# First body's row numbers ahead of the order of the others, a semaphore for each gathered tile, GpSimd without its copies

## The chip, the cores and the metric

One core of a Trainium2 chip runs the kernel. The metric is the time on the device in microseconds (us), the median of three runs. The engines are named as in the profile: PE (TensorE, matmuls), PEld (its weight loads), DVE (VectorE), ACT (ScalarE), POOL (GpSimd), SP (the engine that only starts transfers). A letter q behind an engine's name (PEldq, POOLq) means its sequencer: register work, branches, waits.

## The reference

Two layers on 4 x 512 tokens of width 512, in float32:

```python
x = x + tanh(g_xattn) * xattn(ctx_512, layernorm(x), Wq, Wk, gamma_raw)
x = x + tanh(g_ffn)   * ffn(layernorm(x), gate_w, w1, w2, w3)
# xattn: sim = Q K^T; top 30% of each row kept; A = sigmoid(sim) * mask
#        A = (A + A^T) / 2;  (1 - gamma) * layernorm(x) + gamma * A
# ffn:   each token goes to its 2 best of 8 experts, with softmax weights
#        expert e: w2[e] @ (silu(w1[e] x) * (w3[e] x)), 512 -> 1024 -> 512
```

## The kernel before

The first part (to about 130 us) makes the attention layer, writes the rows with their routing data to a table `found` in HBM, and sorts the tokens by expert. The second part does the experts. Its matmuls take each operand as a high and a low float32r part, three matmuls for one product (L729 to L731).

Two tiles of 128 tokens of expert 0 are done by code written out (`for g in range(WRITTEN)`, g = 0 and 1). All others are done by *bodies*: a loop over experts, and in it a loop over bodies of two tiles of tokens (256 columns), or two and a half where a branch chooses the wide form (320 columns). A body has 8 chunks. Fifteen bodies run here. On PE the branch is `with pe.If(n == wide_at)` (L901): the wide body's code comes first, and the code of the narrow one lies behind it.

A body needs the row numbers of its tiles. PE counts them into PSUM bank 6 (`all_blocks`, L724). DVE turns them into row numbers for all bodies (`order_rows`, L1560 and L1566), copies those of each expert to the place where its bodies begin (`place_rows`, L1577; for experts 1 to 7 it first reads that place from a table), and hands the three row numbers of one body over in `rows_now` (`next_rows`, L1581). POOL waits for that, copies them (`rows_taken`, L525), drains, and starts three indirect DMAs (L528) that bring 128 rows each into `x_body`. All three count up one semaphore, `x_body_in`. ACT waits for all of them and normalises the three tiles (L1082), PE turns them (L754 the two full tiles, L760 the half one), ACT and DVE split the result into high and low parts (L1087, L1092, L1593, L1598), and the last of these sets `xT_body_set`, for which the body's first matmul waits.

For the first body this chain runs beside the second written tile (g = 1). PE's order there is fixed: the turning stands ahead of the last six matmuls of the tile's second layer. `tabulate` on DVE makes the table of bounds that every engine loads before it enters the loops (`table_set`; L331 is that load). SP begins to load expert 1's weights, three transfers of 2 MB (L384), when the first body's rows are there. The results of a body are added to the output by indirect DMAs of POOL (L516 for the written tiles, L534 for bodies); ahead of them it copies the tokens' rows too (`y_row`, L514, L541) and drains (L542).

Of the kernel before, what the change touches and what calls it, by code (L numbers as in the profile page):

```python
# [25 lines left out]
I32 = mybir.dt.int32  # L26
U32 = mybir.dt.uint32
# [4 lines left out]
P = 128  # L32
# [43 lines left out]
FIRST, END, PAIR_TURN, WIDE_AT, THIRD_AT, WIDE_TURN, FRESH_AT, WIDE_SO_FAR, WIDE_IN_ALL = range(9)  # L76
ENTRIES, ENTRY_ROW = 9, 12


def build(nc, x, xT, ctxT, wq_rows, wk_rows, gateT, weights, gains, out):  # L80
# [10 lines left out]
    with stack:  # L91
# [18 lines left out]
        y_row = sb("y_row", [P, 3], I32)  # L110
        no_shift = sb("no_shift", [P, 3], I32)
# [4 lines left out]
        rows_taken = sb("rows_taken", [P, 3], I32)  # L116
# [84 lines left out]
        early_row = sb("early_row", [P, 1], F32, part1)  # L201
        blk_i = sb("blk_i", [P, E], I32, part1)
# [52 lines left out]
        body_rows = scratch[:, TB * N:TB * N + E * BODY_ROWS]  # L255
        row_shift = scratch[:, TB * N + E * BODY_ROWS:TB * N + E * BODY_ROWS + 3 * PLACES].rearrange("p (j c) -> p j c", j=3)
# [13 lines left out]
        UP_BODY, Y_BODY, X_BODY, X_ENTRY, X_LAST = 1, (4, 5, 3), (6, 7), (6, 3), 0  # L270
# [52 lines left out]
        rows_set, x_body_in, x_body_set = sem("rows_set"), sem("x_body_in"), sem("x_body_set")  # L323
# [4 lines left out]
        def entries(eng, e, needed=(FIRST,)):  # L328


            _, values = nc.values_load_multi_w_load_instructions(table[0:1, bass.ds(e * ENTRY_ROW, ENTRIES)], engines=[eng.engine], min_val=0, max_val=MOST,  # L331
                                                                   skip_runtime_bounds_check_because="tabulate() counts bodies, of which there are fewer than MOST")
            bounded = {FIRST: MOST - 1, WIDE_SO_FAR: E}
# [5 lines left out]
        def _(sp):  # L339
# [46 lines left out]
            sp.wait_ge(x_body_in, 48)  # L386
# [4 lines left out]
        def _(pool):  # L391
# [4 lines left out]
            nc.gpsimd.memset(no_shift[:, :], 0)  # L396
# [21 lines left out]
            nc.gpsimd.memset(rows_at[:, :], 0.0)  # L418
# [93 lines left out]
            def add_y(g):  # L512
                pool.wait_ge(y_set, g + 1)
                nc.gpsimd.tensor_tensor(y_row[:, 0:1], token_out[:, 0:1], no_shift[:, 0:1], ALU.add)  # L514
                pool.drain()
                nc.gpsimd.indirect_dma_start(  # L516
                    out, bass.IndirectOffsetOnAxis(ap=y_row[:, 0:1], axis=0), y[:, :], None,
                    bounds_check=TOKENS + 3 * P - 1, oob_is_err=True, compute_op=ALU.add,
                ).then_inc(y_added, 16)

            def gather_body(n):
# [3 lines left out]
                nc.gpsimd.tensor_tensor(rows_taken[:, :], rows_now[:, :], no_shift[:, :], ALU.add)  # L525
                pool.drain()
                for j in range(3):
                    nc.gpsimd.indirect_dma_start(  # L528
                        x_body[:, j, :], None, found, bass.IndirectOffsetOnAxis(ap=rows_taken[:, j:j + 1], axis=0),
                        bounds_check=P + TOKENS + 2 * P - 1, oob_is_err=True,  # L530
                    ).then_inc(x_body_in, 16)

            def add_tile(j, rows, added):
                nc.gpsimd.indirect_dma_start(  # L534
                    out, bass.IndirectOffsetOnAxis(ap=y_row[0:rows, j:j + 1], axis=0), y_tiles[j][0:rows, :], None,
# [43 lines left out]
            pool.wait_ge(x_body_in, end * 48 + 48)  # L579
# [3 lines left out]
        def _(pe):  # L583
# [212 lines left out]
            for g in range(WRITTEN):  # L796
# [69 lines left out]
            with pe.Fori(0, E) as e:  # L866
# [3 lines left out]
                with pe.Fori(of[FIRST], of[END]) as n:  # L870
# [37 lines left out]
        def _(act):  # L908
# [921 lines left out]
```

## Time and profile before

| | us |
|---|---|
| median of three runs (769.46, 771.75, 771.84) | 771.75 |
| the profiled execution, its own time | 769.46 |
| its span, from the first to the last instruction | 767.7 |
| PE busy | 719.1 (94%) |
| DVE, ACT, POOL busy | 398.1, 332.6, 200.5 |

The span and all moments in the rows are those of one profiled execution; 1.8 us of its own time lie outside the span. Since PE is busy for 94% of the span, its idle stretches are what to look for. They lie in the first part, at the entry to the loops (178 to 196 us), and at the end, where POOL adds the last body's result.

### The profile page before, as it was taken

To read this page: it belongs to the slowest core of one execution; us is meant where nothing else is said; L and a number is where in the kernel's file an instruction comes from. 1 tells how busy PE (TensorE), PEld (TensorE's weight loads), DVE (VectorE), ACT (ScalarE), POOL (GpSimd) and SP (SyncE) were. 2 spreads that over 40 slices of the span, in tenths; PEclk is the share of its full clock that TensorE was granted. 3 is DMA by queue.
4 is the path that set the end of the run, shared out by engine and by line. 5 is a ranking of instruction groups with operands and counts; after the bars stand their busy time and mean duration, and the time that the engine had idled before them with its cause. 6 is when DMAs were issued, how large, how long until landed. Compare 5 with 4: busy or idle time off the path is not lost.

```text
span 767.7 us, 13122 instructions
## 1 busy us (share of the span) xinstructions
PE 719.1 (94%) x4507; PEld 620.1 (81%) x4509; DVE 398.1 (52%) x1013; ACT 332.6 (43%) x649; POOL 200.5 (26%) x243
## 2 busy tenths in 40 slices
PE   7698798795999999999999999999999999999994
PEld 3494443574989998999989989999999899989993
DVE  2787779884554355425443564254535542644312
ACT  4797485512454244333533353335333533544221
POOL 4203824972204110403030304030403040203111
PEclk9758999998999999999999999999999999999997
DMA  8972253417516340543226324432363244303122
GB/s 311 411 302 111 110 220 115 138 15 282 178 80 199 121 112 33 135 160 69 109 58 236 69 109 121 166 74 104 62 232 69 109 138 152 67 1 69 42 27 28
DMA packets 24231, 98.76 MB, mean 129 GB/s; under 512 B 4560, under 2 KB 4816, under 8 KB 20368
## 3 DMA queue, kind: packets, MB, share of 16 engines
q1 hardware_dynamic: 14496, 70.54, 23.9%
q0 software_dynamic: 9568, 27.96, 16.1%
q8 instruction: 9, 0.15, 0.1%
q14 instruction: 14, 0.11, 0.0%
q10 hardware_dynamic: 144, 0.00, 0.0%
HBM read 77.50 MB, written 20.99 MB: 128 GB/s over the span
## 4 chain that ended last, share of the span: by engine, by line
issue 67%; POOL 11%; DVE 8%; PE 7%; POOLq 3%; DMA 2%; DVEq 1%; ACT 1%; SPq 0%
POOL x_body L528 4%; POOL out L534 4%; DVE front L1204 2%; POOL xb L474 2%; PE bank L627 1%; PE bank L674 1%; DMA out<-xb 1%; PE bank L600 1%; POOLq L542 1%; PE bank L683 1%; POOLq L331 1%; DVE scratch L1179 1%; PE bank L672 1%; PE bank L590 1%; DMA front<-ctxT 1%
## 5 line engine op out<-in xcount | busy, mean ns | idle before, releaser
L729 PE MATMUL bank<-xT_body_hi,w_hi 128*128 128x256 f32 (+1 forms) x960 | 275.8, 287 | 3.9 <-issue 3.6
L731 PE MATMUL bank<-xT_body_lo,w_hi 128*128 128x256 f32 (+1 forms) x960 | 275.3, 287 | 0.8 <-issue 0.8
L730 PE MATMUL bank<-xT_body_hi,w_lo 128*128 128x256 f32 (+1 forms) x960 | 275.1, 287 | 0.0
L729 PEld LDWEIGHTS bank<-xT_body_hi,w_hi 128*128 128x128 f32 x960 | 181.1, 189 | 10.7 <-issue 5.4
L730 PEld LDWEIGHTS bank<-xT_body_hi,w_lo 128*128 128x128 f32 x960 | 181.5, 189 | 3.6
L731 PEld LDWEIGHTS bank<-xT_body_lo,w_hi 128*128 128x128 f32 x960 | 181.2, 189 | 0.0
L1735 DVE TENSOR_TENSOR h<-bank,act_g 128x256 f32<-128x256 f32 (+1 forms) x120 | 52.4, 437 | 207.5 <-PE bank L731 202.2
L1116 ACT ACTIVATE hT_hi<-h 128x256 fp32r<-128x256 f32 (+1 forms) x120 | 51.4, 428 | 165.6 <-DVE h L1735 165.6
L1369 DVE TENSOR_TENSOR w_lo<-raw,w_hi 128x1024 fp32r<-128x1024 f32 x88 | 105.2, 1223 | 25.0 <-ACT w_hi L958 25.0
L1112 ACT ACTIVATE act_g<-bank 128x256 f32<-128x256 f32 (+1 forms) x120 | 46.5, 388 | 162.2 <-PE bank L731 162.0
L729 PE MATMUL bank<-w_hi,hT_hi 128*128 128x512 f32 (+1 forms) x280 | 114.1, 408 | 1.9 <-DVE hT_lo L1648 1.8
L731 PE MATMUL bank<-w_lo,hT_hi 128*128 128x512 f32 (+1 forms) x280 | 110.2, 393 | 0.0
L730 PE MATMUL bank<-w_hi,hT_lo 128*128 128x512 f32 (+1 forms) x280 | 110.1, 393 | 0.0
L525 POOL TENSOR_TENSOR rows_taken<-rows_now,no_shift 128x3 int32<-128x3 int32 x16 | 3.0, 185 | 350.5 <-DVE rows_now L1581 350.5
L958 ACT ACTIVATE w_hi<-raw 128x1024 fp32r<-128x1024 f32 x88 | 89.1, 1044 | 0.1
L1740 DVE TENSOR_TENSOR hT_lo<-h,hT_hi 128x256 fp32r<-128x256 f32 (+1 forms) x120 | 52.5, 438 | 45.7 <-ACT hT_hi L1116 44.5
L731 PEld LDWEIGHTS bank<-w_lo,hT_hi 128*128 128x128 f32 (+1 forms) x280 | 51.6, 184 | 13.2
L729 PEld LDWEIGHTS bank<-w_hi,hT_hi 128*128 128x128 f32 (+1 forms) x280 | 51.6, 184 | 12.8 <-DVE hT_lo L1648 3.7
L528 POOL DMA_INDIRECT x_body<-found,rows_taken x48 | 51.4, 1070 | 32.3 <-issue 32.3
L730 PEld LDWEIGHTS bank<-w_hi,hT_lo 128*128 128x128 f32 (+1 forms) x280 | 51.8, 185 | 8.9
L1082 ACT ACTIVATE x_body<-x_body 128x512 f32<-128x512 f32 x48 | 35.4, 802 | 5.1 <-DMA x_body<-found,rows_taken 5.1
L534 POOL DMA_INDIRECT out<-y_body,y_row x18 | 35.2, 1954 | 5.5 <-issue 5.5
(307 smaller groups left out, 772.1 us busy)
## 6 DMA issues: line engine op xcount, KB each, us to landing
raw<-weights SPq DMA_DIRECT2D x24, 2048.0 KB, 10.4
raw<-xT SPq DMA_DIRECT2D x4, 1024.0 KB, 11.6
xb<-x SPq DMA_DIRECT2D x4, 1024.0 KB, 20.2
w_hi<-weights POOLq DMA_DIRECT2D x2, 2048.0 KB, 14.9
found<-xb SPq DMA_DIRECT2D x4, 1024.0 KB, 4.5
out<-xb SPq DMA_DIRECT2D x4, 1024.0 KB, 6.9
found<-scratch SPq DMA_DIRECT2D x1, 2092.0 KB, 30.2
front<-ctxT SPq DMA_DIRECT2D x4, 256.0 KB, 4.6
```

The lines of the kernel that those rows point to most:

```text
L528: nc.gpsimd.indirect_dma_start(x_body[:, j, :], None, found, bass.IndirectOffsetOnAxis(ap=rows_taken[:, j:j + 1], axis=0), bounds_check=P ...
L534: nc.gpsimd.indirect_dma_start(out, bass.IndirectOffsetOnAxis(ap=y_row[0:rows, j:j + 1], axis=0), y_tiles[j][0:rows, :], None, bounds_chec ...
L729: nc.tensor.matmul(out_ap, hi, hi_w, start=start, stop=False)
L730: nc.tensor.matmul(out_ap, lo, hi_w, start=False, stop=False)
L731: return nc.tensor.matmul(out_ap, hi, lo_w, start=False, stop=stop)
L958: nc.scalar.activation(w_hi[q][:, j, :], raw[:, q, j * OPW:(j + 1) * OPW], ACT.Copy).then_inc(hi_set[q], 1)
L1082: last = nc.scalar.activation(x_body[:, j, 0:D], x_body[:, j, 0:D], ACT.Identity, bias=x_body[:, j, SHIFT:SHIFT + 1], scale=x_body[:, j, S ...
L1112: nc.scalar.activation(act_g[:, k % 2, 0:cols], bank[GATE[k % 2]][:, 0:cols], ACT.Silu).then_inc(silu_chunk, 1)
L1116: nc.scalar.activation(h_chunk_hi[:, k % 3 * WIDE_COLS:k % 3 * WIDE_COLS + cols], h[:, k % 2, 0:cols], ACT.Copy).then_inc(h_chunk_high, 1)
L1369: V.tensor_tensor(w_lo[q][:, j, :], raw[:, q, j * OPW:(j + 1) * OPW], w_hi[q][:, j, :].bitcast(F32), ALU.subtract).then_inc(lo_set[q], 1)
L1735: V.tensor_tensor(h[:, k % 2, 0:cols], bank[UP_BODY][:, 0:cols], act_g[:, k % 2, 0:cols], ALU.mult).then_inc(h_chunk, 1)
L1740: V.tensor_tensor(h_chunk_lo[:, at], h[:, k % 2, 0:cols], h_chunk_hi[:, at].bitcast(F32), ALU.subtract).then_inc(h_chunk_set, 1)
```

## The change

The diff, cut to its core (the semaphores' and buffers' declarations and the renumbered constants are left out):

```diff
@@ table and entries: one number more for each expert
+FIRST, ..., WIDE_IN_ALL, ROWS_FROM = range(10)
+ENTRIES, ENTRY_ROW = 10, 12
-        rows_at = sb("rows_at", [P, 3 * (MOST + 2) + BODY_ROWS])
+        body_rows = sb("body_rows", [P, (E + 1) * BODY_ROWS], I16)
-        UP_BODY, Y_BODY, X_BODY, X_ENTRY, X_LAST = 1, (4, 5, 3), (6, 7), (6, 3), 0
+        UP_BODY, Y_BODY, X_BODY, X_ENTRY, X_LAST = 1, (4, 5, 3), (6, 7), (1, 3), 0
@@ SP
-            sp.wait_ge(x_body_in, 48)
+            sp.wait_ge(x_body_in[2], 16)
@@ POOL
             def add_y(g):
                 pool.wait_ge(y_set, g + 1)
-                nc.gpsimd.tensor_tensor(y_row[:, 0:1], token_out[:, 0:1], no_shift[:, 0:1], ALU.add)
-                pool.drain()
                 ... the indirect DMA, now with token_out
             def gather_body(n):
                 pool.wait_ge(rows_set, n + 1)
-                nc.gpsimd.tensor_tensor(rows_taken[:, :], rows_now[:, :], no_shift[:, :], ALU.add)
-                pool.drain()
+                pool.sem_inc(let, 1)
                 for j in range(3):
                     ... the indirect DMA, now with rows_now
-                    ).then_inc(x_body_in, 16)
+                    ).then_inc(x_body_in[j], 16)
             def add_body(n):
                 pool.wait_ge(y_set, n)
-                nc.gpsimd.tensor_tensor(y_row[:, :], token_out[:, :], no_shift[:, :], ALU.add)
-                pool.drain()
+                pool.sem_inc(let, 1)
@@ PE, the written tiles
-                    if k == OPS - 1 and g + 1 < WRITTEN:
+                    if k == OPS - 2 and g + 1 < WRITTEN:
                         transpose_x(nth + 1)
-                    elif k == OPS - 1:
+                    if k == OPS - 1 and g + 1 == WRITTEN:
                         pe.wait_ge(x_body_set, 1)
                         turn_pair(X_ENTRY)
+                        pe.wait_ge(x_third_set, 1)
                         turn_last()
@@ PE, in a body
                                 pe.wait_ge(x_body_set, next_nth)
+                                pe.wait_ge(x_third_set, next_nth)
                                 turn_pair(X_BODY)
@@ ACT
             def normal_body(n):
-                act.wait_ge(x_body_in, n * 48 + 48)
                 for j in range(3):
+                    act.wait_ge(x_body_in[j], n * 16 + 16)
                     last = nc.scalar.activation(...)
-                last.then_inc(x_body_set, 1)
+                    if j > 0:
+                        last.then_inc((x_body_set, x_third_set)[j - 1], 1)
@@ DVE
+            def entry_rows():
+                first = rows_ps[:, WRITTEN:WRITTEN + 3]
+                dve.wait_ge(rows_mm, 2)
+                V.scalar_tensor_tensor(entry_shift[:, :], first, 0.0, pad_row[:, :], ALU.is_equal, ALU.mult)
+                dve.drain()
+                V.scalar_tensor_tensor(rows_now[:, :], first, float(P - 1), entry_shift[:, :], ALU.add, ALU.add).then_inc(rows_set, 1)
-            def place_rows(experts):
-                ... a table load, a copy and a drain for each expert
-            def next_rows(n):
-                V.tensor_copy(rows_now[:, :], rows_at[:, bass.ds(n * 3, 3)]).then_inc(rows_set, 1)
+            def next_rows(body):
+                V.tensor_copy(rows_now[:, :], body_rows[:, bass.ds(body * 3, 3)]).then_inc(rows_set, 1)
@@ DVE, tabulate
+                V.scalar_tensor_tensor(rows_from, expert_no[:, :], float(BODY_ROWS // 3), first, ALU.mult, ALU.subtract)
+                V.memset(rows_from[:, 0:1], float(WRITTEN // 2))
@@ DVE, order of the calls
+            slots(0, range(PICKS // 2))
             x_low(2)
-            slots(0)
+            slots(0, range(PICKS // 2, PICKS))
             ...
             product(0, 2, 2 * OPS)
-            order_rows()
-            place_rows([0])
-            next_rows(0)
+            entry_rows()
             h_low(0, 2)
             product(1, 2, 2 * OPS)
             h_low(1, 2)
             tabulate()
-            place_rows([1])
             pair_low(0, 1, X_ENTRY)
             pair_low(1, 2, X_ENTRY)
             last_low(3)
+            order_rows()
             scale_y(0, 1, 2 * OPS)
-            place_rows(range(2, E))
@@ DVE, in a body
-                        next_rows(nth)
+                        next_rows(next_expert if turn else next_here)
```

DVE now works out the first body's three columns alone, and orders the rest after it has split the first body's tiles. On DVE, from the first product of the second written tile (L1644) on, before (`rows_mm` is PE's count of rows, `hhi_set` and `silu_set` are ACT's):

```order
L1644 TENSOR_TENSOR h<-bank,act_g 128x512 [waits piece_done0,silu_set0]
L1560 TENSOR_SCALAR scratch<-bank,pad_row 128x144 [waits rows_mm]
L1560 TENSOR_SCALAR scratch<-bank,pad_row 128x144 x2
L1561 MEMSET scratch 128x216
L1566 SCALAR_TENSOR_TENSOR scratch<-bank,scratch 128x72 x2
L1566 SCALAR_TENSOR_TENSOR scratch<-bank,scratch 128x8x8
L1577 COPY rows_at<-scratch 128x24
L1581 CAST rows_now<-rows_at 128x3
```

And now:

```order
L1644 TENSOR_TENSOR h<-bank,act_g 128x512 [waits piece_done0,silu_set0]
L1562 SCALAR_TENSOR_TENSOR entry_shift<-bank,pad_row 128x3 [waits rows_mm]
L1564 SCALAR_TENSOR_TENSOR rows_now<-bank,entry_shift 128x3
L1648 TENSOR_TENSOR hT_lo<-bank,hT_hi 128x512 [waits hhi_set0]
L1644 TENSOR_TENSOR h<-bank,act_g 128x512 [waits piece_done1,silu_set1]
L1648 TENSOR_TENSOR hT_lo<-bank,hT_hi 128x512 [waits hhi_set1]
```

Eight instructions from the product to `rows_now` have become three. Further on, on DVE from the end of the table to the second tile's output (L1653), before:

```order
L1552 CAST table<-scratch 1x9x8
L1576 TENSOR_LOAD table [waits table_set]
L1576 ISA x2
L1577 ISA
L1577 COPY rows_at<-scratch 128x27
L1593 TENSOR_TENSOR xT_body_lo<-bank,xT_body_hi 128x2x256 [waits x_body_hi] x2
L1598 TENSOR_TENSOR xT_body_lo<-bank,xT_body_hi 128x4x64 [waits x_body_hi]
L1653 TENSOR_SCALAR y<-bank,meta_now 128x512 [waits y_added,piece_done2]
```

And now:

```order
L1554 CAST table<-scratch 1x10x8
L1593 TENSOR_TENSOR xT_body_lo<-bank,xT_body_hi 128x2x256 [waits x_body_hi,table_set]
L1593 TENSOR_TENSOR xT_body_lo<-bank,xT_body_hi 128x2x256 [waits x_body_hi]
L1598 TENSOR_TENSOR xT_body_lo<-bank,xT_body_hi 128x4x64 [waits x_body_hi]
L1570 TENSOR_SCALAR scratch<-bank,pad_row 128x144 x3
L1575 SCALAR_TENSOR_TENSOR body_rows<-bank,scratch 128x72 x2
L1575 SCALAR_TENSOR_TENSOR body_rows<-bank,scratch 128x8x8
L1653 TENSOR_SCALAR y<-bank,meta_now 128x512 [waits y_added,piece_done2]
```

The table load and the copy are gone from between the table and the split, and the order of all rows stands behind the split. On POOL, from the first written tile's addition on, before:

```order
L514 TENSOR_TENSOR y_row<-token_out,no_shift 128x1 [waits y_set]
L516 DMA out<-y,y_row 2432x512
L525 TENSOR_TENSOR rows_taken<-rows_now,no_shift 128x3 [waits rows_set]
L528 DMA x_body<-found,rows_taken 128x523 x3
L514 TENSOR_TENSOR y_row<-token_out,no_shift 128x1 [waits y_set]
L516 DMA out<-y,y_row 2432x512
L556 UNCONDITIONAL_BRANCH [waits table_set]
```

And now (drains and semaphore steps are not in these lists):

```order
L513 DMA out<-y,token_out 2432x512 [waits y_set]
L524 DMA x_body<-found,rows_now 128x523 [waits rows_set]
L524 DMA x_body<-found,rows_now 128x523 x2
L513 DMA out<-y,token_out 2432x512 [waits y_set]
L551 UNCONDITIONAL_BRANCH [waits table_set]
```

The copies no longer stand between a wait and its DMAs.

## Rows read from the trace of the kernel before

**Rows 1.** Waits on PE, 150 to 200 us: total, times, longest.

```profile
PE bank L729 <- issue: 3.6, 1, 3.6
PE bank L754 <- ACT x_body L1082: 3.5, 1, 3.5
PE bank L731 <- issue: 0.8, 1, 0.8
```

**Rows 2.** Waits on PE from 195 us to the end, columns as above.

```profile
PE bank L754 <- ACT x_body L1082: 3.4, 4, 0.8
```

**Rows 3.** Timeline of PE: start, us, engine, line, operation, idle time before and releaser.

```profile
181.44 1.09 PE L754 MATMUL bank<-ident,x_body 128*128 128x128 f32 x8 [3.54 <-ACT x_body L1082]
182.47 0.54 PE L760 MATMUL bank<-ident,x_body 64*128 64x64 f32 x4
...
189.43 0.50 PE L729 MATMUL bank<-xT_body_hi,w_hi 128*128 128x256 f32 x1 [3.56 <-issue]
```

**Rows 4.** PE's sequencer by line: ns min/median/max, first and last start.

```profile
L866 PEldq MOVE  x1: 44/44/44, 181.5 to 181.5; - x1
L901 PEldq COMPARE_BRANCH  x18: 75/206/5947, 183.2 to 719.5; - x18
```

**Rows 5.** DMA queues, 182.7 to 186.7 us, the weights' own: packets, MB, share.

```profile
q1 hardware_dynamic: 119, 1.72, 102.2%
```

**Rows 6.** DMA queues, 186.7 to 189.4 us, the instruction queue alone.

```profile
q8 instruction: 1, 0.02, 2.2%
```

**Rows 7.** Timeline of DVE, columns as in rows 3.

```profile
157.06 0.17 DVE L1586 COPY meta_next<-xtile 128x8 f32<-128x8 f32 x1 [1.92 <-ACT xT_hi L1006]
...
157.98 4.39 DVE L1442 TENSOR_SCALAR scratch<-from_one,slot,number 128x128 f16<-128x128 f16 x16
...
168.72 0.92 DVE L1560 TENSOR_SCALAR scratch<-bank,pad_row 128x144 f32<-128x144 f32 x3 [0.67 <-PE bank L724]
...
170.80 0.17 DVE L1581 CAST rows_now<-rows_at 128x3 int32<-128x3 f32 x1
...
180.14 0.27 DVE L1552 CAST table<-scratch 1x72 int32<-1x72 f32 x1
...
183.21 1.29 DVE L1593 TENSOR_TENSOR xT_body_lo<-bank,xT_body_hi 128x512 fp32r<-128x512 f32 x2 [1.81 <-ACT xT_body_hi L1087]
184.41 0.42 DVE L1598 TENSOR_TENSOR xT_body_lo<-bank,xT_body_hi 128x256 fp32r<-128x256 f32 x1
```

**Rows 8.** Timeline of POOL at the first body's gathers and at the end.

```profile
172.76 1.10 POOL L528 DMA_INDIRECT x_body<-found,rows_taken  x1 [1.52 <-issue]
...
175.49 1.01 POOL L528 DMA_INDIRECT x_body<-found,rows_taken  x1 [0.30 <-issue]
...
758.73 0.19 POOL L541 TENSOR_TENSOR y_row<-token_out,no_shift 128x3 int32<-128x3 int32 x1 [25.41 <-DVE token_out L1621]
759.97 1.56 POOL L534 DMA_INDIRECT out<-y,y_row  x1 [1.05 <-issue]
```

**Rows 9.** POOL's drains by line, columns as in rows 4.

```profile
L542 POOLq DRAIN  x15: 457/1815/5113, 233.2 to 758.7; - x15
L526 POOLq DRAIN  x16: 448/453/5177, 171.0 to 721.1; - x16
```

**Rows 10.** Timeline of ACT and of SP's queue.

```profile
179.17 2.22 ACT L1082 ACTIVATE x_body<-x_body 128x512 f32<-128x512 f32 x3 [5.06 <-DMA x_body<-found,rows_taken]
...
179.48 1.42 SPq L384 DMA_DIRECT2D raw<-weights  x3
```

**Rows 11.** Busy time of PE, PEld, DVE, ACT, POOL (instructions) by window, PEclk, DMA share, GB/s.

```profile
182.70:186.10 3.40, 3.17 (x10) 1.95 (x8) 1.82 (x4) 1.24 (x3) 0.00 (x0) 0.50 1.04 436
186.10:189.50 3.40, 0.07 (x1) 0.08 (x1) 1.09 (x5) 0.00 (x0) 1.55 (x2) 1.00 0.97 410
189.50:192.90 3.40, 3.40 (x16) 3.40 (x17) 0.54 (x3) 0.38 (x1) 0.24 (x1) 0.51 1.03 439
192.90:196.00 3.10, 2.32 (x20) 2.23 (x19) 1.50 (x7) 1.36 (x2) 0.19 (x1) 0.99 1.03 374
```

More of the change, by code:

```diff
@@ L26 @@
 I32 = mybir.dt.int32
+I16 = mybir.dt.int16
 U32 = mybir.dt.uint32
@@ L75 @@
 NEVER = float(MOST)
-FIRST, END, PAIR_TURN, WIDE_AT, THIRD_AT, WIDE_TURN, FRESH_AT, WIDE_SO_FAR, WIDE_IN_ALL = range(9)
-ENTRIES, ENTRY_ROW = 9, 12
+FIRST, END, PAIR_TURN, WIDE_AT, THIRD_AT, WIDE_TURN, FRESH_AT, WIDE_SO_FAR, WIDE_IN_ALL, ROWS_FROM = range(10)
+ENTRIES, ENTRY_ROW = 10, 12
 def build(nc, x, xT, ctxT, wq_rows, wk_rows, gateT, weights, gains, out):
@@ L322, in build @@
         more_pads_in = sem("more_pads_in")
-        rows_set, x_body_in, x_body_set = sem("rows_set"), sem("x_body_in"), sem("x_body_set")
+        rows_set, x_body_set, x_third_set = sem("rows_set"), sem("x_body_set"), sem("x_third_set")
+        let = sem("let")
+        x_body_in = [sem(f"x_body_in{j}") for j in range(3)]
         x_body_mm, x_last_mm, x_body_hi, xT_body_set = sem("x_body_mm"), sem("x_last_mm"), sem("x_body_hi"), sem("xT_body_set")
@@ L328, in entries @@
         def entries(eng, e, needed=(FIRST,)):
-            _, values = nc.values_load_multi_w_load_instructions(table[0:1, bass.ds(e * ENTRY_ROW, ENTRIES)], engines=[eng.engine], min_val=0, max_val=MOST,
+            _, values = nc.values_load_multi_w_load_instructions(table[0:1, bass.ds(e * ENTRY_ROW, ENTRIES)], engines=[eng.engine], min_val=0, max_val=MOST + E * BODY_ROWS // 3,
                                                                    skip_runtime_bounds_check_because="tabulate() counts bodies, of which there are fewer than MOST")
-            bounded = {FIRST: MOST - 1, WIDE_SO_FAR: E}
+            bounded = {FIRST: MOST - 1, WIDE_SO_FAR: E, ROWS_FROM: E * BODY_ROWS // 3}
             return [nc.s_assert_within(v, 0, bounded[k]) if k in needed else v for k, v in enumerate(values)]
@@ L417, in _ @@
             nc.gpsimd.memset(least[:, :], 2.0)
-            nc.gpsimd.memset(rows_at[:, :], 0.0)
+            nc.gpsimd.memset(body_rows[:, :], 0)
             pool.drain()
@@ L513, in add_y @@
                 pool.wait_ge(y_set, g + 1)
-                nc.gpsimd.tensor_tensor(y_row[:, 0:1], token_out[:, 0:1], no_shift[:, 0:1], ALU.add)
-                pool.drain()
                 nc.gpsimd.indirect_dma_start(
-                    out, bass.IndirectOffsetOnAxis(ap=y_row[:, 0:1], axis=0), y[:, :], None,
+                    out, bass.IndirectOffsetOnAxis(ap=token_out[:, 0:1], axis=0), y[:, :], None,
                     bounds_check=TOKENS + 3 * P - 1, oob_is_err=True, compute_op=ALU.add,
@@ L524, in gather_body @@
                 pool.wait_ge(rows_set, n + 1)
-                nc.gpsimd.tensor_tensor(rows_taken[:, :], rows_now[:, :], no_shift[:, :], ALU.add)
-                pool.drain()
+                pool.sem_inc(let, 1)
                 for j in range(3):
                     nc.gpsimd.indirect_dma_start(
-                        x_body[:, j, :], None, found, bass.IndirectOffsetOnAxis(ap=rows_taken[:, j:j + 1], axis=0),
+                        x_body[:, j, :], None, found, bass.IndirectOffsetOnAxis(ap=rows_now[:, j:j + 1], axis=0),
                         bounds_check=P + TOKENS + 2 * P - 1, oob_is_err=True,
-                    ).then_inc(x_body_in, 16)
+                    ).then_inc(x_body_in[j], 16)
             def add_tile(j, rows, added):
                 nc.gpsimd.indirect_dma_start(
-                    out, bass.IndirectOffsetOnAxis(ap=y_row[0:rows, j:j + 1], axis=0), y_tiles[j][0:rows, :], None,
+                    out, bass.IndirectOffsetOnAxis(ap=token_out[0:rows, j:j + 1], axis=0), y_tiles[j][0:rows, :], None,
                     bounds_check=TOKENS + 3 * P - 1, oob_is_err=True, compute_op=ALU.add,
@@ L578, in _ @@
             pool.wait_ge(y_added, end * 32 + 48)
-            pool.wait_ge(x_body_in, end * 48 + 48)
+            for j in range(3):
+                pool.wait_ge(x_body_in[j], end * 16 + 16)
             pool.wait_ge(third_added, wide_in_all * 16 + 16)
@@ L1433, in slots_and_columns, with slots @@
                 V.tensor_scalar(slot[:, q, :, :], slot[:, q, :, :], 1.0, None, ALU.add)
-            def slots(q):
+            def slots(q, picks=range(PICKS)):
                 dve.wait_ge(early_row_mm, 2 + q)
                 dve.drain()
-                for m in range(PICKS):
+                for m in picks:
                     t = PAIR * q + m // 2
@@ L1443, in slots @@
                                            ALU.is_equal, ALU.mult)
-                last.then_inc(slot_set, 1)
+                if m == PICKS - 1:
+                    last.then_inc(slot_set, 1)
             def weights_of(q):
@@ L1495, in tabulate @@
             def tabulate():
-                first, end, pair_turn, at, third_at, wide_turn, fresh_at, so_far, in_all = (table_f[:, E * k:E * (k + 1)] for k in range(ENTRIES))
+                first, end, pair_turn, at, third_at, wide_turn, fresh_at, so_far, in_all, rows_from = (table_f[:, E * k:E * (k + 1)] for k in range(ENTRIES))
                 V.memset(blk_1[:, :], 1.0)
@@ L1724, in _ @@
                 before_e = dve.snap(e - 1)
+                next_expert = dve.snap(e * (BODY_ROWS // 3) + BODY_ROWS // 3)
+                rows_from = of[ROWS_FROM]
                 with dve.Fori(of[FIRST], of[END]) as n:
```

21 lines of the change are left out of this document (5 added, 16 removed).

## The prediction

> **What bounds the kernel now.** I read the page first: PE is busy for 94% of the span, so only what shortens an idle stretch of PE, or the end behind PE, can change the time. The list of waits, cut to the entry of the loops, has three idle stretches that matter: 3.5 us for ACT's normalised rows, 3.6 us and 0.8 us under "issue", that is, for nothing that the profile names [rows 1]. In the loops PE waits for the same rows of ACT four times, 0.8 us each [rows 2]. The reader is to see that the change aims at the first stretch, and to ask what ends the second.
>
> The timeline of PE places them. PE stops at 181.44 - 3.54 = 177.9, turns the rows at 181.44, does its last six matmuls, stops again at 189.43 - 3.56 = 185.9, and starts the first body at 189.43 [rows 3]. The second stretch is no wait for data: the last split of the turned rows ends on DVE at 184.41 + 0.42 = 184.8 [rows 7], 4.6 us before the body starts. PE's sequencer shows what it is. The sequencer runs ahead of the matmuls. It enters the loop at 181.5 (L866), and at 183.2 takes the branch on L901, which jumps over the code of the wide body. That branch takes 5.95 us once, 0.21 us in the median of 18 [rows 4]; 183.2 + 5.95 = 189.2, and 0.2 us later the first matmul starts. Meanwhile the DMA engines are full: the weights' queue alone holds 102% of them from 182.7 to 186.7 [rows 5], and the one packet of 16 KB from the instruction queue q8 starts after 186.7, in the window before PE resumes [rows 6]. I read the branch as a fetch of code, held back by the 6 MB of weights that SP began at 179.48 [rows 10].
>
> This bears on a statement of the Trainium skill, page "Runtime: NRT & Kernel Launch", section "Instruction fetch mechanics": a taken branch whose target isn't in the engine's loaded pages has to fetch that page by DMA before execution goes on. The trace agrees for the first pass (5.95 us); taken for every pass it would be wrong here, as the median of 0.21 us shows.
>
> So the entry has two chains. One is rows_now, gather, normalise, turn. The other is the table, the load of its numbers, the branch, the code. The second decides when the first body starts.
>
> **The change part by part.** *x_low(2) behind eight of the sixteen slots.* The sixteen take 4.39 us, eight 2.2 us. DVE stood idle for 1.92 us, from 155.14 to 157.06, then worked on x_low until the slots at 157.98 [rows 7]. Now it does eight slots from 155.15 to 157.35 and then x_low, 0.9 us, to 158.3. PE's turn of the tile stands one step earlier, so ACT's part is ready long before. Cost: PE starts the second tile some 0.35 us later, and all behind it on PE shifts by that.
>
> *entry_rows for order_rows, place_rows and next_rows.* From the start at 168.72 to the end of rows_now at 170.97 are 2.25 us [rows 7]; two instructions of three columns with a drain between take about 0.45 us (rows_now itself is 0.17 us, the longest small one there 0.27). Less 1.8 us, plus the shift of 0.35: rows_now stands at 169.5.
>
> *No copy and no drain on POOL.* From rows_now at 170.97 to the first gather at 172.76 are 1.79 us [rows 7, 8]. The drain takes 0.45 us in the median and 5.2 us at most [rows 9]; here it began with the copy and took about 0.95 us of it. 0.85 us remain for starting the DMA. Bounds: 0.3 us (the gap between two gathers) and 1.79. With 0.85 the gathers start at 170.4, 171.7 and 173.1 (1.36 us apart). ACT began 3.7 us after the third one's start, so the third lands at 176.8. POOL's addition of the first written tile before it loses its copy too and is out of the way by 168.5.
>
> *A semaphore for each tile.* ACT normalises tile by tile, 0.75 us each: the third is ready at 177.6, the second before that. PE asks for the pair at 177.9 + 0.35 = 178.3. The stall of 3.54 us is gone with 0.7 us to spare, 2 us for the pair; even the upper bound of POOL's start (0.94 us more) leaves only 0.3 us of wait for the half tile.
>
> *What is late next.* PE turns (1.5 us, 181.44 to 182.95) and does its six matmuls (182.95 to 185.9 at half the clock, so 1.5 us at the whole) until 181.3 [rows 3, 11]. The table ends on DVE at 180.41 [rows 7]; it was never behind the old rows' work on PE's path, since DVE waited for ACT before it, so it shifts by 0.35 and by one instruction and one memset more (0.15): 180.9. That is now the last thing for which the sequencer waits, where before it entered at 181.5. The load and the registers up to the branch took 183.2 - 181.5 = 1.7 us; one number more is loaded with the rest. The branch is taken at 182.65 instead of 183.2. Turned rows are split by DVE from 180.95 on, 1.62 us, to 182.6: not late.
>
> *The code fetch.* SP starts the weights when the third tile is in, so at 177.1 instead of 179.48. They need some 14 us at the 410 to 440 GB/s of the windows [rows 11], so they fill the DMA engines until 191.5, before as after around the branch. I take the same 5.95 us. Bounds: 0.2 us (the median) and 7.9 (a third more for a worse place in the queue). The first body starts at 182.65 + 5.95 + 0.2 = 188.8 instead of 189.43: **-0.6 us**. The lower bound is held by the split: 182.8, -6.6 us; the upper gives +1.3 us.
>
> *The clock.* Both idle stretches are followed by a stretch at 1.2 GHz (granted 0.50 and 0.51), 3.4 us each [rows 11]. The first one, over the last six matmuls, is no longer on the path: the sequencer waits for the table. The second costs 3.4 us x (1 - 16/28.8) = 1.5 us, with 16 matmuls in 3.4 us there and 20 in 2.32 behind it, so 0.118 us for one at 2.4 GHz. I expect it again after an idle stretch of 7.6 us: 0.
>
> *The third stretch* (0.8 us, L731, 5.6 us into the body) has the form of a second fetch. The weights end 2.4 us earlier and the body starts 0.6 us earlier, so it meets a fuller or an emptier queue about as before: -0.1, bounds -0.8 and +1.
>
> *The rest of DVE's work.* order_rows now stands behind the splits (1.6 us, its parts of 0.92 and 0.53 us with drains), and the table loads of `place_rows` with their copies, which stood between the second tile and the loops, are gone. From 182.6 on: 1.6 us of order, 0.9 us for the tile's output, some 2.5 us of loads and copies at the loop's head, so 187.6. The first product is needed when two groups of 12 matmuls are done, 4 us behind 188.8: hidden by the code fetch. If that cover goes (a body at 182.8), DVE is 0.8 us late.
>
> *In the bodies.* PE's turn still waits for all three tiles, and ACT's order is the same, so the four waits of 0.8 us stay [rows 2]. The copies and drains on POOL (up to 5.1 us) stand before gathers for which ACT waited once in all, in the first body [rows 10]. The only POOL work in the open is the last: from the copy's start at 758.73 to its DMA at 759.97 are 1.24 us, of which the drain is 0.46 [rows 8, 9]; **-0.4 us**, bounds 0 and -0.9. Two more waits of ACT and one of PE's sequencer in each body stand where both engines have work queued: 0.
>
> Sum: -0.6 - 0.1 - 0.4 = **-1.1 us**. Of 769.46 us for the profiled execution this leaves 768.4; on the median of 771.75 it is 770.6, and I forecast 770.5 for the median.
>
> **Rivals.** *A. The code comes sooner.* The 5.95 us are part queue, part fetch: over 3.5 us pass before q8's packet starts [rows 4, 6]. If after the change the packet finds no such queue (the weights then being 5.5 us under way instead of 3.7), 2.4 us are left: the body starts at 185.3, -4.1; the third stretch goes as well, -0.8; with the end -5.3 us, 766.5 us. For it: the two idle stretches are the same size only by chance. Against: the DMA share is 0.97 to 1.04 all the way [rows 11], and 5 of 6 MB are still queued.
>
> *B. The stall goes and takes its sum with it.* Without the branch's chain one would book the whole 3.54 us, and 0.5 us at the end: 767.7 us. Against: the sequencer entered at 181.5 although the table stood at 180.4, so only 0.6 us can be had unless the table comes sooner.
>
> *C. Slower, by the clock.* PE now idles once for 7.6 us instead of twice for 3.5 us. If the first body then runs at 1.2 GHz for two stretches of the size in rows 11 instead of one, it pays 1.5 us more, and the sum is +0.4 us: 772.2. It decides from 1.1 us on, that is, from nine matmuls more at the low clock. For it: 0.50 and 0.51 after idling of 3.5 us. Against: at 193 the clock was back after 3.5 us of dense work, whatever stood before it. The Trainium skill, page "TensorE: Matmul & The Clock Gate", section "Part 1: The HAM clock gate (the "warmup" mystery)", calls the low state the default, which "activity releases"; by that the work after the idling counts, not its length, and rival C is wrong, as rows 11 hint.
>
> *D. The gathers come no sooner,* because the time ahead of the first was POOL's start and no drain. Then the third lands at 177.7, ACT ends at 178.5, PE waits 0.3 us off the path: the forecast stands.
>
> **How the numbers follow.** A measurement of this kernel tells 0.3%, 2.3 us, from no change. Forecast with D 0.6, A 0.18, B 0.1, C 0.12. Of the forecast's 0.6, 0.04 fall below 769.4 and 0.04 above 774.1, by the spread of the runs (2.4 us among three) and the bound of the fetch; A and most of B (0.24 in all) are faster; of C 0.05 is slower. Faster 0.28, same 0.63, slower 0.09. The forecast's own range is 768.8 to 772.3. The range that holds the time 8 times in 10 reaches to A's 766.5 and to 772.5.
>
> **What would show it.** L754 (L750 now) starts without idle time at about 178.3; the load of the table (L331) on PE at 181.0; the branch (L899 now) at 182.7 with some 6 us; one idle stretch of 7.6 us ahead of the first body; granted clock of 0.5 for one stretch of 3.4 us behind it; POOL's first gather at 170.4; about 0.8 us from token_out to the last addition. Wrong would be: a branch of 2 to 3 us (A), one taken before 182 (B, or the table sooner), two stretches at the low clock (C), or a wait of DVE's first product for its own loads.

## The result, and the profile after

The changed kernel takes 777.99 us in the median of 4 runs (777.12 to 779.04), the kernel before 771.66 on the same chip. The ratio is 1.0086, 95% interval 1.0072 to 1.0101: slower by 0.9%, where 770.5 us and no change had been forecast. The profiled execution takes 777.12 us with a span of 775.3, that is 7.6 us of span more than before.

The entry of the loops came out as forecast. First the timeline of PE, columns as in [rows 3], then PE's sequencer on the branch, as in [rows 4]:

```profile
177.86 1.03 PE L750 MATMUL bank<-ident,x_body 128*128 128x128 f32 x8
178.82 0.46 PE L756 MATMUL bank<-ident,x_body 64*128 64x64 f32 x4
...
188.96 0.58 PE L725 MATMUL bank<-xT_body_hi,w_hi 128*128 128x256 f32 x1 [8.09 <-issue]
```

```profile
L899 PEldq COMPARE_BRANCH  x18: 75/205/6260, 182.4 to 720.8; - x18
```

The turn starts without a wait, where 3.54 us stood before; two idle stretches of 3.5 us have become one of 8.09, and it still ends with the branch, now 6.26 us. The first body starts 0.47 us sooner. One trace can't carry so small a difference: in three more kernels whose code is the same up to there (those of 771.70, 776.82 and 769.59 us below) the first body starts at 190.32, 188.65 and 188.37. The stalls and the branch are what the traces agree on. The timelines of DVE and POOL show why the turn doesn't wait: the row numbers stand at 169.2 and the gathers start at 170.12, where it was 170.97 and 172.76 in [rows 7, 8].

```profile
168.81 0.16 DVE L1562 SCALAR_TENSOR_TENSOR entry_shift<-bank,pad_row 128x3 f32<-128x3 f32 x1 [2.36 <-PE bank L720]
169.05 0.16 DVE L1564 SCALAR_TENSOR_TENSOR rows_now<-bank,entry_shift 128x3 int32<-128x3 f32 x1
```

```profile
170.12 1.10 POOL L524 DMA_INDIRECT x_body<-found,rows_now  x1 [2.08 <-DVE rows_now L1564]
...
172.85 1.01 POOL L524 DMA_INDIRECT x_body<-found,rows_now  x1 [0.30 <-issue]
```

The windows, columns as in [rows 11], show one stretch at 1.2 GHz (granted 0.50 and 0.52), half of it over idle time, and the full clock from 192.9 on, as before.

```profile
182.70:186.10 3.40, 0.00 (x0) 0.00 (x0) 1.62 (x6) 0.00 (x0) 0.36 (x1) 0.97 1.00 429
186.10:189.40 3.30, 0.44 (x2) 0.45 (x3) 0.66 (x3) 0.00 (x0) 2.32 (x2) 0.50 1.00 415
189.40:192.90 3.50, 3.50 (x19) 3.50 (x19) 0.00 (x0) 0.39 (x1) 2.03 (x2) 0.52 1.02 382
192.90:196.00 3.10, 2.66 (x24) 2.46 (x22) 1.39 (x5) 1.52 (x3) 0.00 (x0) 1.00 1.00 336
```

So the loss is elsewhere. PE turns the rows of the next body while it works on a body, so the starts of these turns measure the progress through the loops. There are sixteen; the last one turns rows for which no body comes. The third turn and the last, on PE's timeline, of before and then of after:

```profile
249.25 1.04 PE L754 MATMUL bank<-ident,x_body 128*128 128x128 f32 x8
...
742.87 1.04 PE L754 MATMUL bank<-ident,x_body 128*128 128x128 f32 x8
```

```profile
249.89 1.04 PE L750 MATMUL bank<-ident,x_body 128*128 128x128 f32 x8
...
743.88 1.04 PE L750 MATMUL bank<-ident,x_body 128*128 128x128 f32 x8
```

The second turn (of the second body's rows) still stood 0.65 us ahead (213.43 against 214.08); at the third it is 0.64 us behind, at the last 1.01. One step loses 1.3 us, the thirteen after it 0.4. The last matmul ends 1.1 us late; the other 6.5 us of the 7.6 come behind it. Last of all, each engine's sequencer closes with a drain in the block's exit. These are POOL's, before and after (columns as in [rows 4], the first number one of a single drain, in ns):

```profile
L91 POOLq DRAIN  x1: 216/216/216, 767.2 to 767.2; - x1
```

```profile
L92 POOLq DRAIN  x1: 7010/7010/7010, 768.1 to 768.1; - x1
```

The reader is to see that this drain starts only 0.9 us later than before and takes 6.8 us longer. It waits for no data: every transfer has landed, since POOL waits for their semaphores ahead of it. The two last additions in front of it are as quick as before:

```profile
760.62 1.55 POOL L530 DMA_INDIRECT out<-y,token_out  x1 [28.23 <-DVE token_out L1621]
762.47 1.56 POOL L530 DMA_INDIRECT out<-y_body,token_out  x1 [0.30 <-issue]
```

### The profile page after: what moved, and what is told of

Same layout as the page of the kernel before. It is cut to its first block, busy times and chain, and to the rows that moved or that the text cites. A ratio compares the mean times of both kernels' runs of the same rounds, so it can differ in the third digit from the quotient of the medians.

```text
span 775.3 us, 13095 instructions
## 1 busy us (share of the span) xinstructions
PE 718.8 (93%) x4508; PEld 616.9 (80%) x4509; DVE 397.4 (51%) x1007; ACT 332.3 (43%) x649; POOL 190.7 (25%) x209
## 4 chain that ended last, share of the span: by engine, by line
PE 75%; DVE 9%; issue 5%; ACT 3%; DMA 3%; DVEq 2%; POOL 1%; SPq 0%; ACTq 0%; POOLq 0%
PE bank L725 22%; PE bank L727 22%; PE bank L726 22%; DVE front L1203 2%; PE bank L750 2%; PE bank L623 1%; PE bank L670 1%; ACT x_body L1080 1%; DMA out<-xb 1%; PE bank L596 1%; PE bank L679 1%; DVE w_lo L1368 1%; DVE scratch L1178 1%; ACT w_hi L956 1%; PE bank L756 1%
## 5 line engine op out<-in xcount | busy, mean ns | idle before, releaser
L524 POOL DMA_INDIRECT x_body<-found,rows_now x48 | 50.3, 1049 | 415.4 <-DVE rows_now L1581 403.6
L530 POOL DMA_INDIRECT out<-y,token_out x15 | 29.9, 1990 | 53.5 <-DVE token_out L1621 52.3
L612 PE MATMUL bank<-gate_c,raw 128*128 128x9 f32 x128 | 27.4, 362 | 6.0 <-issue 6.0
```

The lines of the kernel that those rows point to most:

```text
L524: nc.gpsimd.indirect_dma_start(x_body[:, j, :], None, found, bass.IndirectOffsetOnAxis(ap=rows_now[:, j:j + 1], axis=0), bounds_check=P + ...
L530: nc.gpsimd.indirect_dma_start(out, bass.IndirectOffsetOnAxis(ap=token_out[0:rows, j:j + 1], axis=0), y_tiles[j][0:rows, :], None, bounds_ ...
```

## The experiments

The kernel before, beside which these ran, took 770.5 to 770.8 us in the median. "Closing drain" is the one just shown; POOL starts 85 indirect DMAs in the whole program.

**Only POOL's copies and drains taken out of the kernel before.** DVE's code and the entry stay.

```diff
-                nc.gpsimd.tensor_tensor(y_row[:, :], token_out[:, :], no_shift[:, :], ALU.add)
-                pool.drain()
+                pool.sem_inc(let, 1)
                 ... (the same in gather_body, and in add_y without the sem_inc; IndirectOffsetOnAxis reads token_out, rows_now)
```

`let` is a semaphore for which nobody waits.

> The kernel before, with POOL's copies and drains taken away and nothing else changed. Theory 1 (the price of the change is POOL's closing drain, which took 7.0 us after the change and 0.2 before, since no drain stands among the 85 indirect DMAs any more): the closing drain takes about 7 us, PE's entry to the loops is that of before (stalls of 3.5 and 3.6 us, first body at 189.4), and the time is 6 to 7 us over before, 777.5 to 778.5. Rival (the closing drain waits for something in the new row numbers, semaphores or the table): the drain stays at 0.2 us and the time is 771 or less.

Measured: 776.75 us, ratio 1.0078 (1.0057 to 1.0100). Closing drain:

```profile
L91 POOLq DRAIN  x1: 7010/7010/7010, 769.0 to 769.0; - x1
```

The 7.01 us are there without any other part of the change: they come from the removed copies and drains. The next runs tell the two apart. From the second turn (215.55) to the third (251.52) this kernel took 35.97 us, 0.8 more than before.

**One drain ahead of the last addition of the changed kernel,** where POOL has nothing to do for 28 us.

```diff
+            pool.drain()
             add_body(end + WRITTEN)
```

> The changed kernel with one drain on POOL ahead of its wait for the last body's result, where it idles for 28 us. Theory 1: the early drain takes the 7 us, hidden; the closing one takes 0.2 us; 6.8 us less than the changed kernel, 771.2. Rival (the closing drain is long for its place at the end, or waits for the last two additions): it stays at 7 us and the time at 778.

Measured: 771.70 us in the median of 10, ratio 1.0007 (0.9991 to 1.0024). The early drain, then the closing one:

```profile
L568 POOLq DRAIN  x1: 8141/8141/8141, 733.0 to 733.0; - x1
```

```profile
L92 POOLq DRAIN  x1: 225/225/225, 769.6 to 769.6; - x1
```

The work is not gone but hidden (call it a debt that each indirect DMA leaves for the next drain), and 6.3 us of the median come back with one line. What is left of the change is no gain.

**A tensor instruction in place of that one drain,** in the changed kernel, with no drain:

```diff
+            nc.gpsimd.tensor_tensor(spare[:, :], spare_in[:, :], spare_in[:, :], ALU.add)
             add_body(end + WRITTEN)
```

> The changed kernel with one small tensor instruction on POOL at the place of the drain of the run before, and no drain. Theory 1 (it is the drain that settles the indirect DMAs): the closing drain stays at about 7 us. Rival (any compute instruction of POOL behind its DMAs does): it falls to 0.2 us.

Measured, in one run: 782.51 us.

```profile
L92 POOLq DRAIN  x1: 7010/7010/7010, 773.5 to 773.5; - x1
```

It is the drain that retires the debt; a tensor instruction of POOL, like the copies that went, doesn't. In this one run twelve of the fifteen steps from turn to turn also took 0.1 to 0.8 us longer than in the changed kernel; why is open.

**A drain once ahead of the loops,** behind `add_y(1)` of the changed kernel.

> The changed kernel with one drain on POOL ahead of the loops, behind 7 of the 85 indirect DMAs. If the closing drain costs by the number of DMAs since the last one, it takes 78/85 of 7.0 us, 6.4 us; if it costs the same whenever the last drain is long ago, 7.0 us; if it needs only one drain somewhere, 0.2 us. PE's entry to the loops should stay (branch of 6 us).

Measured, in one run: 776.82 us.

```profile
L550 POOLq DRAIN  x1: 11732/11732/11732, 185.3 to 185.3; - x1
```

```profile
L92 POOLq DRAIN  x1: 6438/6438/6438, 768.4 to 768.4; - x1
```

Seven of the 85 DMAs stood ahead of the first drain (two gathers of the written tiles, the first body's three, two additions), so 78 ahead of the second: 6.44 us / 78 = 0.0825 us each. In the changed kernel 7.01 / 85 = 0.0825 too. With 2 DMAs since the last drain it takes 0.22 us. All three points lie on one line, 0.06 us and 0.082 us for each DMA. Whether it is the DMAs that count or their packets isn't separated, since nearly all of them move 128 rows. The drain of 8.14 us above had 83 DMAs behind it, 6.9 us by this line; its last DMA had started 0.4 us earlier, and what the other 1.3 us are isn't separated. The first of the two drains here is far longer than seven DMAs explain; what such a drain waits for shows further below.

**PE's If turned round,** in the kernel with the early drain: the code of the narrow body stands first, where the wide one's stood.

```diff
-                    with pe.If(n == wide_at):
-                        body(WIDE_COLS, WIDE_TILES)
+                    with pe.If(n != wide_at):
+                        body(PAIR_COLS, PAIR_TILES)
                     with pe.Else():
-                        body(PAIR_COLS, PAIR_TILES)
+                        body(WIDE_COLS, WIDE_TILES)
```

> The changed kernel with one drain ahead of the last addition (as in the run before this one, 771.7 us), and TensorE's If in the loop of the bodies turned round: narrow body in the first branch, wide body in the other. Theory (the stall ahead of the first body is the fetch of code behind the first jump over the wide body): the first body's branch, 6.26 us in the changed kernel, falls to under 1 us, the idle stretch ahead of the first body from 8.1 to 2 to 3 us (the table's load at 181.07 is then last), the first body starts at 183 to 185, and the time falls by 4 to 5.5 us to 766 to 767.5; the fetch may come back smaller at the first wide body. Rival 1 (the fetch is paid whatever lies where, since nothing of the loop was run before): branch or the matmul behind it still waits some 6 us, time 771 to 772. Rival 2 (the clock eats it, the earlier start falls into a stretch at 1.2 GHz): start at 184 but under 2 us gained, 770.

Measured: 767.65 us in the median of 7, ratio 0.9960 (0.9945 to 0.9974): the best of the study, 3.0 us below before and 4.05 below its twin with the If as it was (771.70). The branch by PE's sequencer, and PE's waits from 150 to 240 us (total, times, longest):

```profile
L900 PEldq COMPARE_BRANCH  x27: 66/169/3747, 183.3 to 752.2; - x27
```

```profile
PE bank L726 <- issue: 3.6, 1, 3.6
PE bank L726 <- DVE xT_body_lo L1599: 1.9, 1, 1.9
```

The first body now waits 1.9 us for its data and starts at 183.73. The jump is paid one body later. At the end of the first body the sequencer jumps over the wide body's code, which now lies behind the narrow one's: that is the branch of 3.75 us, at 218.9. PE stands for 3.65 us ahead of the second body, which is narrow too:

```profile
225.38 0.38 PE L726 MATMUL bank<-xT_body_hi,w_hi 128*128 128x256 f32 x1 [3.65 <-issue]
```

Behind this idle stretch the granted clock is 0.60 for 3.5 us, with 19 matmuls in them. The third body, the first wide one, begins at 261.95 without a wait. Against the twin, the first step from turn to turn is 7.06 us shorter and the second 4.04 longer, so the moved jump is worth 3.0 us. The other 1.0 come in the steps of bodies 8, 12 and 14 (35.0 us for 35.4), and why is open.

**The same turn of the If in the kernel before,** and nothing else.

> The kernel before with TensorE's If turned round and nothing else. Before: turn of the last stage waited until 181.44, branch 5.95 us at 183.4, first body at 189.4. Theory of the code fetch: the first body then starts when the matmul behind the branch can, about 184, so 5 us are gained: 765.5 to 767. And since the row numbers are then the last to come (turn 181.44), the changed kernel's earlier rows would only here begin to be worth their 3 us: the run of the changed kernel with the same turn should start its first body 2 to 3.5 us ahead of this one, unless the table's load (180.9) holds it. Rival (fetch paid whatever lies where): 770 to 771.5.

Measured: 776.04 us, ratio 1.0065 (1.0047 to 1.0082), *slower* by 5.4 us. PE's waits from 150 to 240 us, and the last of DVE's copies of row numbers (L1577) with what follows it:

```profile
PE bank L754 <- ACT x_body L1082: 4.7, 2, 3.8
PE bank L729 <- DVE h L1735: 4.5, 1, 4.5
PE bank L729 <- issue: 3.5, 1, 3.5
```

```profile
188.06 0.18 DVE L1577 COPY rows_at<-scratch 128x27 f32 x1
...
192.88 0.18 DVE L1577 COPY rows_at<-scratch 128x27 f32 x1 [0.78 <-issue]
194.94 0.17 DVE L1625 COPY weight_body<-x_body 128x3 f32 x1 [1.88 <-issue]
...
195.55 0.42 DVE L1735 TENSOR_TENSOR h<-bank,act_g 128x256 f32<-128x256 f32 x1
```

Both theories on record missed. The first body does start without the branch, at 187.09, but six copies at 0.97 us each (a load of the table, a copy and a drain) hold DVE until 193, and PE stands 4.5 us for its first product. These copies are what the change removes from the entry. Under the old branch they were covered. Now the first step from turn to turn takes 33.37 us, 0.7 more than before: the copies take back all that the branch gave. And the jump still comes at the end of the first body (3.77 us at 227.5, the 3.5 us under "issue"), with a granted clock of 0.66 for 3.5 us behind it: the second step takes 40.40 us, 5.2 more than before. The wait for the row numbers (3.8 us) is there too. The two kernels with the If turned round are 8.4 us apart: that is what the change, with its one early drain, is worth once its cover is off.

**The drains kept, the copies gone,** in the changed kernel: `pool.drain()` behind both `pool.sem_inc(let, 1)`.

> The changed kernel with a drain in each body's gather and each body's addition, as before the change, but still without the copies. Theory 1 (the closing drain pays about 82 ns for each indirect DMA since the last drain): closing drain falls from 7.01 to 0.2 us, 777.99 to 771.2. Theory 2 on top of it (the 1.29 us lost between body 1 and body 2 come from GpSimd's additions that run undrained beside VectorE's wait for semaphores): that gap falls by 0.8 us as it did rise by in the kernel that only lost copies and drains, time 770.3 to 770.7. Rival (the 1.29 us come from the longer table and its loads on VectorE): gap stays at 1.2 to 1.3, time 771.2 to 771.7. Rival to all (drains cost in the bodies, as they wait for landings): 772 or more, with PE waiting for DMA rows in the bodies.

Measured: 769.67 us in the median of 10, ratio 0.9982 (0.9969 to 0.9995). POOL's drains ahead of the gathers and of the additions:

```profile
L523 POOLq DRAIN  x16: 212/213/10496, 170.2 to 721.8; - x16
```

```profile
L539 POOLq DRAIN  x15: 213/1862/5612, 235.5 to 759.1; - x15
```

The first row gives the line one more point: behind two additions this drain takes 0.21 us, behind the three of a wide body 0.29. From the second turn to the third the kernel takes 35.62 us (36.46 in the changed kernel), and to the last 528.3 (530.45). DVE's waits over the second body, 218 to 246 us, here and in the changed kernel:

```profile
DVE weight_body L1627 <- issue: 5.5, 1, 5.5
```

```profile
DVE weight_body L1625 <- issue: 5.5, 1, 5.5
...
DVE h L1735 <- remote: 2.7, 1, 2.7
```

Before, the first of these rows was 3.3 us and the second did not exist. The 2.7 us under "remote" (a semaphore from another engine that came late) go with the drains, and the kernel that had only lost copies and drains shows 2.7 us of it on ACT. The 5.5 us stay, and the kernel with DVE's old code and no drains on POOL shows 3.1 in this row: they belong to DVE's part of the change, the longer table entry and the code around it. The table entry itself is the smaller part: DVE's load of it takes 1.07 us for ten numbers and 0.85 for nine. That the 5.5 us cost the 0.45 us that are left is by elimination.

**Both together: drains kept and If turned round.**

> The changed kernel with the drains in the bodies (as in the run of 769.67 us) and TensorE's If turned round (as in the run of 767.65 us). Theory (two separate effects: with the If turned round the far jump comes in a later body and costs 3.75 instead of 6.3 us; the drains space GpSimd's DMAs, so that waits of 0.4 us in three bodies and about 0.8 us ahead of the second body's turn go): 769.67 - 4.05 = 765.6, between 765 and 766.5. Rival (the two share one cause, the late semaphores around GpSimd's DMAs at the entry): 767 to 768.

Measured: 774.49 us, ratio 1.0045 (1.0029 to 1.0062). POOL's drain ahead of the gathers, and PE's wait at the second turn:

```profile
L523 POOLq DRAIN  x16: 205/213/10353, 170.9 to 725.9; - x16
```

```profile
PE bank L752 <- ACT x_body L1082: 5.4, 1, 5.4
```

Neither theory had it. At 189.0 this drain starts behind the addition of 187.30, which lands, behind the weights, 11.8 us after its start, at 199.1. The drain ends 0.3 us later, after 10.35 us, and the second body's gathers stand behind it. In the kernel of 769.67 us, whose first body starts at 190.1, the same drain takes 10.5 us and ends 0.2 us after its addition has landed, and the second turn waits 0.9 us, as in the changed kernel; with a first body some 6 us sooner it waits 5.4.

**The second expert's weights asked for later,** in the kernel with drains kept and the If as it was.

```diff
             sp.wait_ge(x_body_in[2], 16)
+            sp.wait_ge(gate_chunk_mm, 1)
```

> The changed kernel with drains in the bodies, If as it was, and one wait more on the DMA queue's engine: the second expert's weights are asked for only once the first body's first chunk of matmuls is done, some 8 to 10 us later than now. Theory (the first far jump takes 6 us because its code comes through DMA queues that the weights fill, DMA share 0.95 to 1.08 there; with idle queues it took 3.75 in the kernel with the If turned round): branch 3.7 to 4 us instead of 6.54, first body 2.5 us earlier. Rival (the length belongs to the jump's target, not to the load): branch 6 us or more. The time is no test, since the weights come later: 767 to 772.

Measured: 775.19 us, ratio 1.0049 (1.0033 to 1.0065). The branch, and the DMA queues while it lasts (183.6 to 187.2 us):

```profile
L902 PEldq COMPARE_BRANCH  x18: 75/205/3580, 183.4 to 726.2; - x18
```

```profile
q8 instruction: 1, 0.02, 2.0%
q14 instruction: 1, 0.01, 1.0%
```

With nothing else in the queues the same jump to the same code takes 3.58 us, against 6.54. So about 3 us are queueing behind the weights and 3.6 the fetch itself. This agrees with the Trainium skill, page "Runtime: NRT & Kernel Launch", section "Instruction fetch mechanics" (a taken branch to a page not loaded waits for its fetch by DMA), which gives no time. The whole kernel is slower, since PE then waits 6.5 us for a product behind the late weights.

**A drain ahead of the additions alone.**

> The changed kernel with a drain ahead of the additions of each body, none in the gathers. Theory (what costs the bodies 2.1 us between the second body's turn and the last one's is that additions follow the gathers at once, in the bodies ahead of which the gathers come late): turn of second body to turn of last body 528.3 to 528.8 as with both drains, against 530.45 in the changed kernel, closing drain 0.2 us, time 769.5 to 770.5. Rival (the drain in the gathers matters, or any instruction between): 530 or more, time 771 to 772.

Measured: 769.59 us in the median of 10, ratio 0.9985 (0.9975 to 0.9996).

```profile
L538 POOLq DRAIN  x15: 209/1667/5735, 233.1 to 757.3; - x15
```

The same as with both drains, in the time and from the second turn (212.91) to the third (248.53), 35.62 us. The drains ahead of the gathers earn nothing.

**The same with the If turned round.**

> The changed kernel with a drain ahead of each body's additions and none in the gathers (as in the run of 769.59 us), and TensorE's If turned round. Theory (the 774.49 us of the kernel with both drains and the If turned round came from the drain ahead of the second gather, 10.35 us under the weights' load, which made the second body's turn wait 5.44 us): here nothing drains between the two gathers at the entry, so the turn comes at 207 to 208 without a wait over 1 us, and the later bodies keep what the drains gave: 769.59 - 4.05 = 765.5, between 764.8 and 766.5. Rival (turning the If round gains only where no drain stands in the loop): 769 or more.

Measured: 768.32 us in the median of 8, ratio 0.9970 (0.9958 to 0.9983). The 5.4 us of the kernel with both drains are gone, so the drain between the two gathers was their cause. But it is no better than with one early drain (767.65): the steps of bodies 8, 12 and 14 take 35.45 us here and 34.95 in its twin with the If as it was, 1.5 us in all, so of the 2.8 us that the moved jump gives only 1.3 are left. The changed kernel has 35.34 to 35.39 us there, the kernel of 767.65 us 35.0 to 35.06, and neither theory says why. It stays open.

## Why the prediction was wrong

*What bounds the kernel, and the two chains:* right. The stall for the row numbers went, and the branch decided the start of the first body.

*x_low, entry_rows, the gathers:* right in each place. The turn was forecast at 178.3 and came at 177.86; rows_now at 169.5, came at 169.2; the first gather at 170.4, came at 170.12. All three came 0.3 to 0.4 us early, for the shift of 0.35 us was hardly there: DVE's wait for PE's rows ended at 168.81, before at 168.72. On DVE two instructions stand from the product to rows_now, where nine stood.

*The code fetch:* 5.95 us taken, 6.26 found (6.54 and 6.32 in the two kernels that have drains in the bodies again); first body forecast at 188.8, found at 188.96, so -0.47 us instead of -0.6. That it came so near is partly luck, as the starts from 188.4 to 190.3 in the other traces show. The tenth number of the table was priced at nothing and costs PE 0.23 us in its load (1.28 us for 1.04 at the entry). That the branch is held back by the weights is now shown. Rival A (code sooner) and rival B (the whole stall) fall: the branch grew.

*The clock:* right, 0. Rival C needed two low stretches in the first body, and the windows show one. Its threshold was also worked out wrongly: at 0.21 us for a matmul at the low clock and 0.118 at the high one, 1.1 us are twelve matmuls more, not nine.

*The third stretch:* 0.44 us for 0.78, so -0.3 against -0.1.

*The rest of DVE's work, "hidden by the code fetch":* right, and the text named the cover. The 0.8 us that it named for a lost cover didn't come: with the If turned round (767.65 us) the first body starts at 183.73 and PE has no row of a wait for DVE's first product, only 1.9 us for the split. What it did not price is the old order without the cover: the run with the If turned in the kernel before shows 4.5 us of wait for DVE's old copies.

*In the bodies:* this is the step that failed, in the sentence "The only POOL work in the open is the last ... -0.4 us, bounds 0 and -0.9". The copy and drain at the end did go: from token_out at 759.56 to the first addition at 760.62 are 1.06 us, from 758.48 to 759.97 they were 1.49, so -0.43. But the drain that every engine does at the block's exit then had 85 DMAs to retire instead of 2: +6.8 us, wholly in the open. The prediction priced the removed drains by what they cost where they stood, and never asked what they had been doing for the drain that stays. The bound of 0 on the upper side had no reason behind it. The "0" for the rest of the bodies missed too: from the second turn to the last the changed kernel takes 530.45 us and the one before 528.79, 1.7 us more; with the drains kept it is 528.3.

With that step repaired the time comes near the sum: 769.67 and 769.59 us in the median with drains kept, 1.0 and 1.2 us below before, where -1.1 was worked out. But that is not the sum of its terms. With the drains kept, the end gives 0.2 us and not 0.4 (1.31 us from token_out to the addition, for 1.49). The second step loses 0.45 us, and the thirteen after it win 0.9; none of these terms was in the forecast. So the agreement is in part luck.

## What to carry to other kernels

A drain that is removed must be priced twice: where it stood, and at the next one that remains, above all the one at the end of the program; where the engine is idle late in the kernel, one drain there hides the debt. When two waits lie over the same time, price each part of a change with the cover off as well: here the same edit to the code's order is worth -4 us with the change and +5.4 us without it.

## What the runs showed of the hardware

POOL's drain takes about 0.082 us for each indirect DMA started since the last one (0.21 to 0.22 us after 2, 0.29 after 3, 6.44 after 78, 7.01 after 85), even when all have landed. It also waits for one still in flight: under the load of 6 MB of weights two such drains took 10.4 and 10.5 us and ended 0.2 to 0.3 us behind the landing of the addition before them. A third took 11.7 us, with no landing on record. A tensor instruction of POOL doesn't do this work: with one in the drain's place the closing drain still took 7.01 us.

PE's first jump over the code of the other body cost 3.5 to 3.8 us with idle DMA queues and 5.8 to 6.5 us with full ones; the median of all such branches is 0.17 to 0.21 us. That the time is a fetch of code is read from the packets of the instruction queues that lie in it.

Without drains between POOL's indirect DMAs, ACT or DVE stood once for 2.7 us in the second body under "<-remote", in the changed kernel and in the one that had only lost POOL's copies and drains; before and with the drains kept there is no such row. But the kernels of 782.51 and 767.65 us have no drain there either, and no such row. So the row isn't tied to the drains alone, and that the indirect DMAs delay the semaphores isn't shown.
